# Attention and FFN layer on one core: first two turns written out, x turned by transposing transfers instead of a second, blocked load

## The reference

```
for each block of 128 rows (8 blocks in each batch), for each of 8 heads:
    q = x Wq, k = x Wk, v = x Wv      (each 64 wide)
    att_mem = (elu(q)+1) @ mem / ((elu(q)+1) @ z)
    mem, z += (elu(k)+1)^T v, sums of (elu(k)+1)
    att = sigmoid(betas) * att_mem + (1 - sigmoid(betas)) * softmax(q k^T / 8) v
y   = layernorm(x + att @ Wo)
out = layernorm(y + relu(y @ W1q^T + b1) @ W2q^T + b2)      W1q, W2q rounded to -1, 0, 1
```

## Time and profile before

| | |
|---|---|
| median of 3 runs | 1892.02 us |
| the profiled execution's own time | 1893.2 us |
| its span, first to last instruction | 1891.4 us |
| PE busy | 1801.1 us (95%) |
| DVE, ACT, POOL busy | 75%, 53%, 41% |
| PE instructions | 15935 |
| HBM | 36 GB/s over the span |

### The profile page before, as it was taken

The page is one execution under the profiler, slowest core; times in us unless marked ns, Lnnn a source line. Parts: engine busy times, 40 slices in busy tenths (PEclk is TensorE's granted clock), DMA queues, the critical chain, the costliest instruction groups (busy, mean ns, idle before and its releaser), DMA issues.

```text
span 1891.4 us, 42414 instructions
## 1 busy us (share of the span) xinstructions
PE 1801.1 (95%) x15935; PEld 1254.6 (66%) x15935; DVE 1424.0 (75%) x2807; ACT 998.7 (53%) x2422; POOL 783.1 (41%) x775
## 2 busy tenths in 40 slices
PE   4689999999999999999999999999999999999998
PEld 3466777666677666677766677766677766667765
DVE  6667777878777777877777877777877777877774
ACT  5665645545654555554555554554564554565441
POOL 0203444533454444344444344443344443344442
PEclk9789999999999999999999999999999999999999
DMA  8524335445425355434445434435433434442220
GB/s 273 141 42 75 74 69 87 57 86 87 84 58 92 55 83 91 84 66 81 69 70 92 85 63 82 76 63 92 85 74 70 84 57 88 88 82 59 58 46 23
DMA packets 555130, 150.87 MB, mean 80 GB/s; under 512 B 528544, under 2 KB 532528, under 8 KB 554416
## 3 DMA queue, kind: packets, MB, share of 16 engines
q1 hardware_dynamic: 554928, 148.16, 41.6%
HBM read 50.54 MB, written 16.80 MB: 36 GB/s over the span
## 4 chain that ended last, share of the span: by engine, by line
PE 69%; ACT 16%; DVE 10%; issue 4%; DMA 1%; POOL 0%; SPq 0%; ACTq 0%; DVEq 0%; POOLq 0%
ACT bank L1137 12%; PE bank L448 12%; PE bank L449 11%; PE bank L464 7%; PE bank L465 7%; PE bank L294 6%; PE bank L295 6%; PE bank L296 6%; PE bank L378 3%; PE bank L428 3%; PE bank L426 3%; PE bank L427 3%; ACT y_rows L1175 2%; DVE exp_bias L742 2%; ACT p_rows L1148 1%
## 5 line engine op out<-in xcount | busy, mean ns | idle before, releaser
L448 PE MATMUL bank<-yt,w1t 128*128 128x256 f16 x2048 | 455.5, 273 | 1.9 <-DVE yt L825 1.9
L449 PE MATMUL bank<-yt,w1t 128*128 128x256 f16 x2048 | 455.5, 273 | 0.0
L464 PE MATMUL bank<-w2t,arena 128*128 128x512 f16 x1024 | 395.8, 387 | 0.0
L465 PE MATMUL bank<-w2t,arena 128*128 128x512 f16 x1024 | 395.2, 386 | 0.0
L1193 ACT ACTIVATE arena<-bank,b_scaled,wscalars 128x256 f32<-128x256 f32 x512 | 261.9, 565 | 242.9 <-PE bank L449 171.8
L1137 ACT ACTIVATE bank<-bank,exp_bias,gscalars 128x128 f32<-128x128 f32 x512 | 220.6, 431 | 225.3 <-DVE exp_bias L742 225.3
L448 PEld LDWEIGHTS bank<-yt,w1t 128*128 128x128 f16 x2048 | 200.8, 98 | 25.4 <-ACT w2t L1218 2.0
L449 PEld LDWEIGHTS bank<-yt,w1t 128*128 128x128 f16 x2048 | 200.9, 98 | 23.3
L865 DVE CAST arena<-arena 128x512 f16<-128x512 f32 x256 | 186.7, 730 | 7.8 <-ACT arena L1193 7.8
L1403 POOL TENSOR_TENSOR arena<-arena 128x512 f16<-128x512 f32 x128 | 155.5, 1215 | 76.3 <-DVE arena L865 76.3
L464 PEld LDWEIGHTS bank<-w2t,arena 128*128 128x128 f16 x1024 | 101.6, 99 | 123.0 <-issue 7.7
(11 more groups left out here) (180 smaller groups left out, 4317.8 us busy)
## 6 DMA issues: line engine op xcount, KB each, us to landing
rows<-in_L_attn_x SPq DMA_DIRECT2D x32, 512.0 KB, 3.8
out_rows<-rows SPq DMA_DIRECT2D x64, 256.0 KB, 2.4
x_blocks<-in_L_attn_x SPq DMA_DIRECT2D x248, 64.0 KB, 3.0
sk<-sk_t SPq DMA_DIRECT2D x480, 32.0 KB, 2.0
arena<-in_L_ffn_W SPq DMA_DIRECT2D x6, 1024.0 KB, 5.5
w2t<-in_L_ffn_W SPq DMA_DIRECT2D x2, 1024.0 KB, 13.4
w1t<-in_L_ffn_W SPq DMA_DIRECT2D x2, 1024.0 KB, 14.2
amax_row<-amax_dram SPq DMA_DIRECT2D x31, 64.0 KB, 3.5
```

Source lines behind the costliest of these rows:

```text
L448: pe.matmul(ps[:, c], w1t[:, k, cols], yt[:, g % 2, :, k], start=k == 0, stop=False)
L449: ins = pe.matmul(ps[:, c], w1t[:, k, cols], yt[:, g % 2, :, KT + k], start=False, stop=k == KT - 1)
L464: pe.matmul(banks[own][:], h_hi[:, f, toks], w2t[:, f, :], start=f == 0, stop=False)
L465: ins = pe.matmul(banks[own][:], h_lo[:, f, toks], w2t[:, f, :], start=False, stop=f == FT - 1)
```

## The change

1. `load_blocks`, the tile `x_blocks` and DVE's `turn_x` are gone. `group_max`, `xt_hi` and `xt_lo` read the rows that `load_x` brings; the halves go to a new tile `x_rows`, and SP turns them with two `dma_start_transpose` a turn (`turn_x`, 128 x 1024 f16 each), from `x_rows` into `xt`.
2. In the loop the scale of the next turn's x is made earlier on each engine: `group_max` behind `h_split(5)`, both bounces ahead of the first `turn_p`, `all_max` and `x_scale` between the pieces of the scores, `xt_hi` and `xt_lo` right behind the v halves.
3. On PE `read_memory` stands behind the first piece of the second `ffn_down` instead of ahead of it.
4. Turns 0 and 1 are written out on PE, DVE, ACT and SP, in another order; the loop starts at g = 2. POOL's code is unchanged.

```diff
-        x_blocks = sb("x_blocks", [P, TG, D])
+        x_rows = sb("x_rows", [P, TG, 2, D], F16)
...
+        def xt_there(g, t):
+            return (sem["xt"], t + 1) if g == 0 else (sem[f"xt{t}"], 16 * g)
...
-                pe.wait_ge(sem["xt"], by_t(g, 1))
+                pe.wait_ge(*xt_there(g, 0))
+                pe.wait_ge(*xt_there(g, 1))
...
+            spread_max(3)
+            sum_all(1)
+            project_v(0, 0)
+            project_v(0, 1)
+            for n in range(0, 4):
+                turn_w(n)
+            attend(0, 0)
+            for n in range(4, 8):
...
+            for n in range(8, 12):
+                turn_w(n)
+            project_qk(1, "k", 0)
+            sum_all(2)
+            turn_att(0, 0)
+            project_qk(1, "k", 1)
+            for n in range(12, 16):
+                turn_w(n)
+            project_qk(1, "q", 0)
...
+            project_out(0, 0)
+            project_out(0, 1)
+            for n in range(20, 24):
+                turn_w(n)
+            update_memory(0, 0)
...
+            for n in range(24, 28):
+                turn_w(n)
+            turn_y(0, 0)
+            turn_y(0, 1)
+            project_v(1, 0)
+            project_v(1, 1)
+            for n in range(28, 32):
+                turn_w(n)
+            ffn_up(0, 0)
+            for g in range(2, NG + 2):
...
                 ffn_up(g - 2, 4)
-                if g == 1:
-                    update_memory(0, 0)
-                    update_memory(0, 1)
+                if g == LIVE:
+                    attend(1, 0)
+                    attend(1, 1)
                 project_qk(g, "k", 0)
...
                 project_v(g, 0)
...
                 project_v(g, 1)
+                ffn_down(g - 2, 1, 0)
                 read_memory(g, 0)
                 read_memory(g, 1)
-                ffn_down(g - 2, 1, 0)
...
-                if g == 0:
-                    dve.wait_ge(s_x[0], 16)
-                else:
-                    dve.wait_ge(sem["xblocks"], 16 * 8 * g)
+                dve.wait_ge(s_x[g % NX], 16 * (g // NX + 1))
...
-                dve.wait_ge(sem["xblocks"], 16 * 8 * g)
-                dve.transpose(x_blocks[:, t], x_blocks[:, t]).then_inc(sem["xturn"], 1)
-
             def xt_lo(g, t):
                 if not 0 <= g < NG:
                     return
                 dve.wait_ge(sem["xt_hi"], by_t(g, t))
-                dve.scalar_tensor_tensor(out=xt[:, t, KT:2 * KT], in0=in_cols(x_blocks, t) if g else x_bank(t), scalar=gcol(g, G_SCALE), in1=xt[:, t, 0:KT],
+                if g:
+                    dve.scalar_tensor_tensor(out=x_rows[:, t, 1], in0=rows[:, g % NX, t], scalar=gcol(g, G_SCALE), in1=x_rows[:, t, 0],
+                                             op0=ALU.mult, op1=ALU.subtract).then_inc(sem["xt_lo"], 1)
+                    return
+                dve.scalar_tensor_tensor(out=xt[:, t, KT:2 * KT], in0=x_bank(t), scalar=gcol(g, G_SCALE), in1=xt[:, t, 0:KT],
...
+            qk_split(1, "k", 0)
+            threshold(2)
+            at_lo(0, 0)
+            round_w(4)
+            qk_split(1, "k", 1)
+            round_w(5)
+            qk_split(1, "q", 0)
+            at_lo(0, 1)
...
+            for g in range(2, NG + 2):
                 qk_split(g, "k", 0)
                 h_split(g - 2, 4)
-                if g == 0:
-                    w_split("q", 1)
                 h_split(g - 2, 5)
+                group_max(g + 1)
                 qk_split(g, "k", 1)
...
-                if g == 0:
-                    gates()
-                group_max(g + 1)
                 p_lo(g, 0, 0)
+                all_max(g + 1)
+                x_scale(g + 1, 0)
                 score_max(g, 1, 0)
+                x_scale(g + 1, 1)
                 p_lo(g, 0, 1)
+                x_scale(g + 1, 2)
                 score_max(g, 1, 1)
-                if g >= LIVE:
-                    mem_add(g - 1, 0)
-                    mem_add(g - 1, 1)
+                x_scale(g + 1, 3)
+                mem_add(g - 1, 0)
+                mem_add(g - 1, 1)
                 p_lo(g, 1, 0)
-                turn_x(g + 1, 0)
-                turn_x(g + 1, 1)
...
                 v_split(g, 1)
+                xt_lo(g + 1, 0)
+                xt_lo(g + 1, 1)
                 read_scale(g, 0)
                 read_scale(g, 1)
                 residual(g - 2, 0, 1)
...
-                all_max(g + 1)
-                x_scale(g + 1, 0)
...
-                x_scale(g + 1, 1)
-                x_scale(g + 1, 2)
-                x_scale(g + 1, 3)
...
                 att_scale(g, 0)
-                xt_lo(g + 1, 0)
                 att_scale(g, 1)
-                xt_lo(g + 1, 1)
...
                 if g:
-                    act.wait_ge(sem["vproj"], by_t(g - 1, t))
-                    act.wait_ge(sem["kproj"], 2 * g)
-                    act.wait_ge(sem["qproj"], 2 * g)
-                act.wait_ge(sem["xturn"], by_t(g, t))
-                act.activation(xt[:, t, 0:KT], in_cols(x_blocks, t) if g else x_bank(t), ACT.Copy, scale=gcol(g, G_SCALE)).then_inc(sem["xt_hi"], 1)
+                    if g > 1:
+                        act.wait_ge(sem[f"xt{t}"], 16 * (g - 1))
+                    act.wait_ge(s_x[g % NX], 16 * (g // NX + 1))
+                    ins = act.activation(x_rows[:, t, 0], rows[:, g % NX, t], ACT.Copy, scale=gcol(g, G_SCALE))
+                else:
+                    act.wait_ge(sem["xturn"], t + 1)
+                    ins = act.activation(xt[:, t, 0:KT], x_bank(t), ACT.Copy, scale=gcol(g, G_SCALE))
+                ins.then_inc(sem["xt_hi"], 1)
...
+            w_sum(2, 0)
+            xt_hi(1, 0)
+            xt_hi(1, 1)
+            for n in range(0, 8):
+                put_w(n)
+            w_sum(2, 1)
+            for n in range(8, 12):
+                put_w(n)
+            qk_split(1, "k", 0)
...
+            exponentials(1, 0, 1)
+            p_hi(1, 0, 1)
+            yt_hi(0, 0)
+            yt_hi(0, 1)
+            for n in range(24, 28):
+                put_w(n)
+            exponentials(1, 1, 0)
...
+            for n in range(28, 32):
+                put_w(n)
+            xt_hi(2, 0)
+            xt_hi(2, 1)
+            h_relu(0, 0)
+            h_relu(0, 1)
+            h_relu(0, 2)
+            h_relu(0, 3)
+            for g in range(2, NG + 2):
...
                 v_split(g, 1)
...
+                xt_hi(g + 1, 0)
+                xt_hi(g + 1, 1)
...
-                xt_hi(g + 1, 0)
...
                 h_relu(g - 1, 0)
                 h_relu(g - 1, 1)
-                xt_hi(g + 1, 1)
                 h_relu(g - 1, 2)
...
-            def load_blocks(g):
...
-                if g > 1:
-                    sp.wait_ge(sem["xt"], by_t(g - 1, 1))
-                for t in range(TG):
-                    src = x[b0 + t, seg * P:(seg + 1) * P, :].rearrange("(b j) (k a i) -> a j k b i", j=32, a=4, i=32)
-                    for a in range(4):
-                        dst = x_blocks[32 * a:32 * a + 32, t].rearrange("p (k b i) -> p k b i", k=KT, b=4)
-                        sp.dma_start(dst, src[a]).then_inc(sem["xblocks"], 16)
+            def turn_x(g, t):
+                if not 0 <= g < NG:
+                    return
+                sp.wait_ge(sem["xt_lo"], TG * (g - 1) + t + 1)
+                sp.wait_ge(sem["kproj"], 2 * g)
+                sp.wait_ge(sem["qproj"], 2 * g)
+                sp.wait_ge(sem["vproj"], by_t(g - 1, t))
+                sp.dma_start_transpose(xt[:, t], x_rows[:, t].rearrange("p c n -> p (c n)")).then_inc(sem[f"xt{t}"], 16)
...
-            for g in range(NG + 2):
-                if g == 1:
-                    load_ffn_w(2, 3)
-                load_blocks(g + 1)
-                if g == 0:
-                    load_ffn_w(2, 0)
+            load_x(1)
...
+            bounce_out(2)
+            turn_p(1, 0)
+            turn_p(1, 1)
+            bounce_back(2)
+            turn_x(2, 0)
+            turn_x(2, 1)
+            move_sk(1)
+            turn_att(1, 0)
...
+            for g in range(2, NG + 2):
                 bounce_out(g + 1)
-                if g == 0:
-                    gates_out()
+                bounce_back(g + 1)
                 turn_p(g, 0)
                 turn_y(g - 1, 0)
                 turn_y(g - 1, 1)
                 turn_p(g, 1)
-                bounce_back(g + 1)
-                if g == 0:
-                    load_ffn_w(2, 1)
-                    gates_back()
+                turn_x(g + 1, 0)
+                turn_x(g + 1, 1)
                 move_sk(g)
                 turn_att(g, 0)
                 turn_att(g, 1)
                 put_out(g - 2, 0)
-                if g == 0:
-                    load_x(1)
                 put_out(g - 2, 1)
-                if g == 0:
-                    load_x(2)
-                    load_ffn_w(2, 2)
-                if g >= 1:
-                    load_x(g + 2)
+                load_x(g + 2)
...
```

(121 more changed lines are left out.)

205 lines of the change are left out of this document (77 added, 128 removed).

## The result

| | before | after |
|---|---|---|
| median of 4 runs, us | 1891.76 (1890.69 to 1892.17) | 2029.79 (2027.72 to 2031.22) |
| ratio, with its 95% interval | 1 | 1.073 (1.0711 to 1.0748) |
| span of the profiled execution | 1891.4 | 2029.0 |
| first k projection of turn 1, of turn 2 | 91.3, 142.3 | 74.7, 139.5 |
| one turn of the loop | 55.9, one in four 57.6 | 61.3 (54.7 the first, then 59.3 to 62.8) |

The change makes the kernel 138 us slower; 1855 was forecast. First the busy time by stretch, start and loop, in the columns of the earlier trace rows (length; busy time of PE, PE's weight loads, DVE, ACT, POOL; granted clock; DMA share; GB/s).

The account below looks back on a forecast made before the run. PE was taken to bound the kernel, its loop idling at `read_memory` for `p_lo`. 1893.2 - 34 (swap) - 3 (start) = 1856.2, less 1.2 to the median: 1855 us, other terms 0; range 1844 to 1867.

Parts of the forecast that it names:

- What bounds the kernel: PE in the loop: nearly all its idle time is at `read_memory`, waiting for DVE's `p_lo`, 34.7 us in 30 waits.
- The swap: On PE, one `ffn_down` piece of 1.73 us ahead of `read_memory` covers the 1.13 wait, 30 times: 34 us off.
- x without the blocked load: Loop: transposing transfers of x, 4.6 us each, are hidden and `group_max` moves free of cost: 0; ends 2.4 and 2 x 4.6.
- The trip of the maximum: Loop, write and read back through DMA ahead of `all_max`: 11.2 us, up to 14.2 free; counted 0, at most 21 in all.
- reserves of 1.3, 1.0 and 0.7: Spare us a turn for that trip: SP's read back ahead, ACT's bias for the third score piece, PE's cover at `read_memory`.
- The start: Turns 0 and 1 reordered: first k projection of turn 1 is 15 us earlier, most given back; 3 off, from 15 kept to 5 lost.
- The rivals: Four other outcomes: wait returns elsewhere, 0.10; start loses, 0.07; longer trip of the maximum, 0.04; wait not for banks, 0.05.
- Rival 1: Loop: PE's wait returns at `read_scale` ahead of `ffn_up` or at the attend step; 1872 to 1889; chance 0.10.
- rival 3: SP's trip of the maximum gets longer ahead of every turn of p; slower from 15.4 us, 1939 at 17; chance 0.04.

Follow-up runs that it names:

- e3: The kernel before with the swap alone: first piece of the second `ffn_down` ahead of `read_memory` on PE; 1841.78 us, ratio 0.9745.
- e1: The changed kernel with SP issuing, in the loop, the `put_out` stores and `load_x` ahead of the two `turn_att`; 1842.56 us, ratio 0.975.
- e4: e1 with the swap on PE taken back, `ffn_down` piece behind `read_memory` again; 1895.85 us, ratio 1.0025 to the kernel before.
- e6: The changed kernel with `group_max` alone moved in the loop, behind the second q split; 1920.36 us, ratio 1.0144 to the kernel before.
- e2: The kernel before with `group_max` alone moved behind `h_split(5)` and reading the rows of `load_x` from turn 3 on; 2176.95 us, ratio 1.152.
- e8: The changed kernel with POOL's `add_bias` (1.41 us) behind the second `at_lo` instead of between the two; 1987.91 us, ratio 1.0504 to the kernel before.
- e5: The changed kernel with `group_max` moved behind `h_split(7)` and `all_max` with `x_scale` behind `v_split(1)`, SP's order untouched; 1844.74 us, ratio 0.9746 to the kernel before.

## Why the prediction was wrong, step by step

**What bounds the kernel: right.** The wait at `read_memory` is what before loses in its loop, and e3 takes it all.

**The swap: the mechanism right, the term too small.** 34 was forecast, 48 measured (e3: 1841.78 against 1890.19). The term counted the wait, 30 x 1.13, and took the busy time of 1600.1 as fixed, though the same row had the clock at 0.99. Without the wait the busy time is 1586.3.

**x without the blocked load: 0, right but for the step that failed.** The two transfers land in 3.3 us at the median (3.1 to 4.3), under the 4.6 taken; e1 and e3 differ by 0.8, less than their intervals (some 3 us each way) tell apart, and without the swap (e4) the x path and the start together cost 0.25%, so they are worth nothing that can be seen.

**The step that failed is the last sentence of that part: "`group_max` (1.21) moves to a place where DVE has just been relieved of its wait for `xt_hi`: 0."** It priced the instruction and the engine's free time, and did not ask whether its input is there. The old `group_max` read `x_blocks`, the new one reads rows, and both moved: the input in what it is, the step by some 15 us in the turn. The rows that would have said so were in hand, the load at 720.45 and the end of `h_split(5)` at 716.37. Priced so, the step would have been 7.9 of waiting in each of 29 turns, with `k_lo` behind it. Put at 0, it measured 187 us: 2029.79 with the load as it stands, 1842.56 with the load moved. The order of SP alone showed the load behind `turn_att` and `put_out`, and it was quoted in the description of the change.

**The trip of the maximum: no loss seen, but its start was taken too early, by the same omission.** In the changed kernel and in e1 `all_max` has no wait for its DMA. The reserve was worked out for a write at 720.84. But the write needs the maximum of those rows, which by the rows of before is there at 724.25 + 1.21 = 725.5 at the earliest, and 4.6 is more than the reserves of 1.3, 1.0 and 0.7 together: by the prediction's own sum this term wasn't 0 either. The changed kernel hides it, since DVE is as late itself; in e1 the load is early enough; e6 finds the wait where it was said to come. The section of the Trainium skill that the prediction names for 2.0 us is on transfers that GpSimd issues, while these are SP's; the rows, 7.7 and 3.5, are what the sum went by.

**The start: the marks met, the second by luck, the worth too high.** The first k projection of turn 1 was forecast at 76 and stands at 74.7, that of turn 2 at 139 and stands at 139.5. But e3, with the old start, has that second mark at 139.7 as well (its edit does nothing in turns 0 and 1, where that `ffn_down` is empty), and e2, with the old start too, at 139.1; the 142.3 of before is one execution's. The 15 gained are given back in full; the 2.8 by which the stretch is shorter than before aren't the rewriting's, and the forecast of 3 was met by luck.

**The rivals.** None was this one. Rival 1 spoke of PE meeting the chain of ACT and DVE at another point, and PE's new waits are of that kind, but its cause and its price were others (17 to 34 us), and rival 3 had another DMA, the trip's and not the load's. All four asked what happens behind the steps the change speaks of; none asked of each moved reader when its writer is done. The chance of slower, 0.05, rested on that omission.

A rule bears on the mechanism. In the trace of the changed kernel SP stands 270.5 us in 59 waits at L1626 for POOL's `at_lo`, with the load behind it:

```profile
SPq L1626 <- POOL att_dot L1457: 270.5, 59, 18.4
```

The Trainium skill, DMA: Bandwidth & Descriptors (Anatomy of one DMA), says that DMA engines don't wait on semaphores: a wait is served by the issuing sequencer before it dispatches. By this rule, the trace agrees, every later transfer of that queue shares the wait, whatever its own data are.

## What to carry to other kernels

For every step that a change moves earlier, or gives another input, find when the writer of that input is done in the trace of before, and compare it with the end of the step it will stand behind; do this for the input's DMA first, since a load stands behind all the waits of its queue. If the writer is later, the wait is not paid once but can close into a ring over the turns, and then every engine's work between the two ends lengthens the turn, idle engines' too (e8: 1.4 us on POOL made 42 us). Here the best kernels are two: the one-line swap (e3), or the whole change with its load ahead of `turn_att` (e1), both at 1842.

## What the hardware showed that was not expected

A wait of 1.13 us once in a turn of 55.9 cost more than itself. In the kernel before and in e4, which both have it, PE's granted clock falls to 1.2 GHz for 3.4 us in one turn of four, some 2 us behind the end of that wait, and that turn is 1.7 us longer with the same matmuls (the two windows under e3). One such stretch of before, with its granted clock of 0.50 behind the counts:

```profile
405.10:408.50 3.40, 3.40 (x10) 1.22 (x9) 3.11 (x10) 0.00 (x0) 1.27 (x1) 0.50 1.30 129
```

In e1, e3 and e5, without the wait, no turn of the loop is longer than 55.6, and the mean clock is 1.00. So this gap had to be priced with the busy time that it costs, not by its length alone: 48 for 35. But it is no rule for every gap. In e6 PE stands still twice as long, 70.0 us in the loop, ahead of L309 and L379, and the clock falls once in 29 turns:

```profile
141.30:1807.40 1666.10, 1596.09 (x14389) 1110.73 (x14386) 1260.21 (x2432) 870.88 (x2144) 698.63 (x700) 1.00 0.38 75
```

Why the one gap lowers the clock and the others don't is not shown.

The Trainium skill, TensorE: Matmul & The Clock Gate (A second HAM failure mode), tells of a kernel whose short but frequent idle times let the clock go down and up again. The kernel before and e4 agree with it in kind, at a mean clock of 0.99; e6, whose gaps are as frequent and longer in sum, doesn't (1.00).
